# A new opening of the feed-forward layer, and another order in the tail, in a kernel of two attention and two feed-forward layers on one Trainium2 core

## The reference

```python
# end of attention 0: normalization of each head, scale, residual
h_norm = (h - mean) * rsqrt(var + 1e-05) * outnorm_scale      # 4 heads of 64
x = x + h_norm
# feed-forward 0, on the layer norm of x; act_qdq takes the largest |x| of the whole tensor
x = act_qdq(_layernorm(x))
up   = act_qdq(x @ lpbq_dequant(w_up).T)
gate = act_qdq(x @ lpbq_dequant(w_gate).T)
...
# experts: router on the layer norm of x, top 2 of 8, places by a running count
router_logits = einsum('gth,he->gte', x, w_router)            # 2 groups of 1024 tokens
gate, idx = top_k(softmax(router_logits), 2)
pos = cumsum(mask_kt, axis=1) * mask_kt - 1.0                 # capacity 160
y = combine(relu(expert_in @ wi) @ wo)
```

## Time and profile before

| | |
|---|---|
| median of 3 runs | 592.25 us (591.8 to 594.39) |
| the profiled execution | 594.54 us |
| its span, first to last instruction | 592.8 us |
| busy: TensorE, VectorE, ScalarE, GpSimd | 519.8, 381.6, 327.0, 142.5 us |
| mean granted TensorE clock | 0.952 |
| opening of feed-forward 0 | about 73 to 121 us |
| tail up to the first expert | about 393 to 425 us |

### The profile page before, as it was taken

One profiled execution on the slowest core, in us unless ns is written; L12 is line 12 of the kernel. 1 busy time (PEld: TensorE's weight loads), 2 busy tenths in 40 slices (PEclk: granted clock), 3 DMA queues, 4 the chain that ended last, 5 costly groups with the idle time before them and its releaser, 6 DMA issues.

```text
span 592.8 us, 9394 instructions
## 1 busy us (share of the span) xinstructions
PE 519.8 (88%) x3362; PEld 372.6 (63%) x3362; DVE 381.6 (64%) x980; ACT 327.0 (55%) x697; POOL 142.5 (24%) x202
## 2 busy tenths in 40 slices
PE   1989996899999700999999999998999999999994
PEld 1568864654444300887757678777788777677773
DVE  6576889845389989788688699987732232233101
ACT  2857577723389969680389799997122212211220
POOL 2006544000000000000332232211245344534441
PEclk9989999999999955699999999999799999999998
DMA  7910000000000000016000011014215645353410
GB/s 221 305 19 1 2 1 0 2 0 1 0 0 1 1 0 0 1 46 239 2 0 2 1 39 36 2 37 159 52 46 170 200 132 195 121 181 124 132 46 22
DMA packets 32013, 37.62 MB, mean 63 GB/s; under 512 B 8672, under 2 KB 27744, under 8 KB 31968
## 3 DMA queue, kind: packets, MB, share of 16 engines
q1 hardware_dynamic: 28896, 29.07, 15.3%
q0 software_dynamic: 3072, 7.95, 4.3%
HBM read 30.14 MB, written 6.88 MB: 62 GB/s over the span
## 4 chain that ended last, share of the span: by engine, by line
PE 71%; DVE 14%; ACT 9%; issue 2%; POOL 2%; POOLq 0%; DVEq 0%
PE pA L2203 12%; PE pB L2233 10%; PE pC L1869 6%; PE pC L1908 5%; PE pA L1902 3%; PE pB L1918 3%; PE pC L2217 3%; PE pA L1824 2%; PE pB L1824 2%; PE pC L1824 2%; ACT XIT L748 2%; DVE am L1259 2%; DVE arena L1255 2%; PE pB L1998 2%; DVE am L1225 2%
## 5 line engine op out<-in xcount | busy, mean ns | idle before, releaser
L499 POOL TENSOR_TENSOR arena<-KT,par 128x256 f32<-128x256 f32 x32 | 19.0, 615 | 248.6 <-DVE XIT L1333 186.7
L2203 PE MATMUL pA<-arena 128*128 128x320 f32 (+2 forms) x320 | 75.7, 387 | 0.5 <-ACT arena L923 0.5
L937 ACT ACTIVATE arena<-pA 128x320 f32<-128x320 f32 (+2 forms) x80 | 30.7, 384 | 73.0 <-PE pA L2203 67.5
L2203 PEld LDWEIGHTS pA<-arena 128*128 128x128 f32 x320 | 53.7, 190 | 16.2 <-issue 1.1
L2233 PE MATMUL pB<-arena 128*128 128x256 f32 x256 | 59.8, 385 | 0.0
L2233 PEld LDWEIGHTS pB<-arena 128*128 128x128 f32 x256 | 47.2, 190 | 8.5 <-issue 2.3
L1225 DVE TENSOR_REDUCE am<-arena 128x1 f32<-128x512 f32 x48 | 32.1, 682 | 23.0 <-ACT arena L688 22.9
L1869 PE MATMUL pC<-wdnT,XIT 128*128 128x256 f32 x192 | 43.5, 384 | 0.8 <-DVE XIT L1333 0.8
L1409 DVE TENSOR_REDUCE rm<-pA 128x16 f32<-128x2048 f32 x16 | 36.7, 2291 | 8.8 <-PE pA L1902 8.8
L1869 PEld LDWEIGHTS pC<-wdnT,XIT 128*128 128x128 f32 x192 | 36.5, 193 | 6.9 <-DVE XIT L1333 1.6
L1908 PE MATMUL pC<-ident,arena 128*128 128x128 f32 x240 | 35.4, 280 | 1.5 <-ACT XIT L784 0.8
(11 more groups left out here) (338 smaller groups left out, 1147.2 us busy)
## 6 DMA issues: line engine op xcount, KB each, us to landing
arena<-in_L_ffn_wi SPq DMA_DIRECT2D x8, 1024.0 KB, 5.2
arena<-in_L_ffn_wo SPq DMA_DIRECT2D x8, 1024.0 KB
X<-in_x SPq DMA_DIRECT2D x4, 512.0 KB, 5.7
arena<-in_ctx SPq DMA_DIRECT2D x4, 512.0 KB, 7.3
out<-X SPq DMA_DIRECT2D x4, 512.0 KB, 2.9
token_rows<-arena SPq DMA_DIRECT2D x4, 512.0 KB, 4.7
arena<-in_L_ffn_w_up SPq DMA_DIRECT2D x1, 768.0 KB, 7.5
arena<-in_L_ffn_w_gate SPq DMA_DIRECT2D x1, 768.0 KB, 9.2
```

The costliest lines, as they stand in the source:

```text
L937: nc.scalar.activation(HT[:, e % 2, f, n], ps[2 + f % 2][:, 0:n.stop - n.start], ACT.Relu).then_inc(s["h_relu"], 1)
L2203: last = mm(ps[2 + f % 2][:, 0:n.stop - n.start], WI[:, u, k, f * P:(f + 1) * P], XET[:, u, k, n], start=(k == 0), stop=(k == KD - 1))
```

## The change

In the opening: `head_scale(0)` comes before two `w_round` on VectorE; the fourth head of tiles 8 to 12 goes from VectorE to ScalarE (`ALL_HEADS` = 13); `values_kept(1)` and (2) come after tiles 4 and 9 in place of 6 and 14; `keys(2)` comes after the last head; two weight turns stand before the layer norm; four tiles (`NORM_ACT`) are normalized by ScalarE, by scale and bias; `TURN_BESIDE` is shorter, and the last two weight turns follow the spreading of the maximum, with four identity products instead of eight. In the tail: `d_back` comes directly behind `d_logits`, `d_turn(6)` and `d_turn(7)` earlier, `d_back4` behind `count(0)`; ScalarE takes the last roots and norms sooner; there are seven identity products in place of eleven.

```diff
-        TURN_BESIDE = (0, 2, 4, 5, 7, 8, 10, 11, 13)
+        TURN_BESIDE = (-1, -1, 1, 3, 5, 8, 11)
+
+        NORM_ACT = (4, 7, 10, 13)
 
         HB = NB // 2
+
+        ALL_HEADS = 13
@@ POOL h_scale
-                if b >= HB:
-                    pool.wait_ge(s["last_normed"], b - HB + 1)
+                if b >= ALL_HEADS:
+                    pool.wait_ge(s["last_normed"], b - ALL_HEADS + 1)
@@ ACT head_norm
-                for n in range(NH0 if b < HB else NH0 - 1):
+                for n in range(NH0 if b < ALL_HEADS else NH0 - 1):
@@ ACT, after the heads
-                if b == 13:
-                    keys(2)
+            keys(2)
+            keys(3)
+            weights_copy(4)
             rsqrt(4, NB)
-            keys(3)
+            weights_copy(5)
+
+            def xl_act(b):
+                if b == NORM_ACT[0]:
+                    act.wait_ge(s["xl_scale"], 1)
+                nc.scalar.activation(at(XL, b), at(X, b), ACT.Identity, scale=rstd[:, cols(b, 1)], bias=s2[:, cols(b, 1)]).then_inc(s["xl_act"], 1)
...
             for b in range(NB):
+                if b + 3 in NORM_ACT:
+                    xl_act(b + 3)
                 copy_x(b)
                 if b in TURN_BESIDE:
                     weights_copy(4 + TURN_BESIDE.index(b))
+            weights_copy(11)
+            weights_copy(12)
@@ ACT, tail
             norm4_act(8)
+            rsqrt(9, 4, 12)
             lt_copy()
             norm4_act(9)
-            rsqrt(9, 4, 12)
+            act.wait_ge(s["xr_ready"], 5)
+            norm4_act(12)
+            norm4_act(13)
             xt4(4)
             xt4(5)
+            norm4_act(14)
+            norm4_act(15)
+            xt4(6)
             lt4_copy()
-            act.wait_ge(s["xr_ready"], 5)
-            for b in range(12, NB):
-                norm4_act(b)
             exp4(0)
-            xt4(6)
             xt4(7)
@@ DVE, attention 0
+                if t == NB // 2:
+
+                    head_scale(0)
                 for b in (2 * t - 2, 2 * t - 1):
                     if b >= 0:
                         w_round(b)
-                if t == NB // 2:
-                    head_scale(0)
@@ DVE, opening
-                if HB <= t + 2 < NB:
+                if ALL_HEADS <= t + 2 < NB:
                     last_head(t + 2, 0, 0)
...
-                if t in (6, 14):
-                    values_kept(1 + t // 14)
+
+                if t == 4:
+                    values_kept(1)
+                if t == 9:
+                    values_kept(2)
...
             for t in range(NB + 1):
-                if t < NB:
+                if t < NB and t not in NORM_ACT:
                     xl(t, 0, 0)
+                if t == 1:
+                    V_.scalar_tensor_tensor(out=s2[:, 0:NB], in0=mean[:, 0:NB], scalar=-1.0, in1=rstd[:, 0:NB], op0=ALU.mult, op1=ALU.mult).then_inc(s["xl_scale"], 1)
@@ PE (turn3 and xl_max wait on xl_act for the tiles of NORM_ACT)
+            weights_turn(4)
+            weights_turn(5)
             for b in range(NB):
                 turn3(b)
                 if b in TURN_BESIDE:
...
-            pe.wait_ge(s["wtr_copied"], 13)
...
             whole_max(0, 1)
-            keep_busy(ps[1], 8)
+
+            weights_turn(11)
+            weights_turn(12)
+            keep_busy(ps[1], 4)
+            pe.wait_ge(s["wtr_copied"], 13)
@@ PE, tail
             d_logits()
+            d_back()
             d_turn(4)
-            d_back()
             d_turn(5)
             keep_busy(ps[7], 2)
+            d_turn(6)
             d_logits4()
+            keep_busy(ps[7], 2)
+            d_turn(7)
             keep_busy(ps[7], 3)
-            d_back4()
-            keep_busy(ps[7], 4)
...
-            d_turn(6)
-            keep_busy(ps[7], 2)
-            d_turn(7)
             count(0)
+            d_back4()
             for b in range(12, NB):
                 d_row(b)
```

More of the change, by code:

```diff
@@ L1200, in xl_max @@
             def xl_max(b, u, h):
-                dve.wait_ge(s["xl_ready"], b + 1)
+                if b in NORM_ACT:
+                    dve.wait_ge(s["xl_act"], NORM_ACT.index(b) + 1)
+                else:
+                    dve.wait_ge(s["xl_ready"], b + 1 - sum(r < b for r in NORM_ACT))
                 V_.tensor_reduce(am[:, 0, cols(b, 1)], at(XL, b), AX.X, ALU.max, apply_absolute_value=True).then_inc(s["xl_max"], 1)
             for t in range(NB + 1):
-                if t < NB:
+                if t < NB and t not in NORM_ACT:
                     xl(t, 0, 0)
+                if t == 1:
+                    V_.scalar_tensor_tensor(out=s2[:, 0:NB], in0=mean[:, 0:NB], scalar=-1.0, in1=rstd[:, 0:NB], op0=ALU.mult, op1=ALU.mult).then_inc(s["xl_scale"], 1)
                 if t >= 1:
@@ L1786, in turn3 @@
             def turn3(b):
-                pe.wait_ge(s["xl_ready"], b + 1)
+                if b in NORM_ACT:
+                    pe.wait_ge(s["xl_act"], NORM_ACT.index(b) + 1)
+                else:
+                    pe.wait_ge(s["xl_ready"], b + 1 - sum(r < b for r in NORM_ACT))
                 if b >= 2:
```

## The result

The changed kernel takes 588.65 us (median of nine runs, 587.62 to 591.66) against 592.25 (nine runs, 591.74 to 594.39): ratio 0.9933 [0.9917, 0.995]; the medians lie 3.6 us apart. The whole interval lies at or beyond the 0.5% that the prediction set as the bound, so the kernel is faster by it. Its profiled execution took 589.84 us with a span of 588.1, against 594.54 and 592.8.

A forecast was written before the change was run, and what follows sets the result against it. TensorE, busy 88%, was taken as the bound, so gains could come only where it waits: the feed-forward opening (2.5 us) and the tail (1.1), together 3.6 off 592.25, giving 588.65 us; range 587.2 to 590.9.

The forecast's parts named there:

- rival A: Whole kernel: gains come as summed, 588.65 us, own range 587.6 to 589.6; chance 0.50.
- Step (1): Opening: head_scale(0) ahead of two w_round; ScalarE's first head 1.8 us sooner, heads 3 and later 1.0 us sooner.
- no wait of ScalarE's variance beyond 0.3 us: Opening: a listed sign that the prediction is right, limiting ScalarE's wait for the variance to 0.3 us.
- Step (2): Opening: five fourth heads move to ScalarE, keys(2) behind the last head; last addition on VectorE 1.3 us sooner.
- Step (3): Opening: values_kept earlier, values(3) at full clock; ScalarE's keys and weight copy hidden by 0.2 us, first normalization 1.3 sooner.
- Step (4): Opening: four of 16 normalizations go to ScalarE; gain 1.2 us, ScalarE's tiles ready 1 to 2 us early.
- rival C: Opening: ScalarE becomes the limit, opening gives 1.2 us and tail 1.1; 590.0 us, chance 0.12.
- Step (5): Opening's end: last two weight turns behind the spread maximum, four identity products for eight; same length, ending with x_int(0).
- Rival B: Gate products: low clock there costs 1.7 us, leaving a gain of 1.9; 590.35 us, chance 0.27.
- Steps (6) and (7): Tail: last roots ahead of lt_copy and d_back ahead of d_turn(4); logits_0 0.95 us sooner.
- Steps (8) and (9): Tail: exp4(0) ready in time by 0.1 to 0.2 us, count(0) earlier; find_places(0) 1.1 us sooner in all.
- Rival D: Tail: low clock of 417 to 424 moves off the identity products, half of 2.9 us more; 587.2, chance 0.07.

The follow-up runs named there:

- scale_back: Changed kernel with head_scale(0) put back behind the two w_round; 589.2 us in its one run.
- ahead: Changed kernel with two more weight turns and their copies moved ahead of the layer norm; 594.23 us, ratio 0.9994 to the kernel before.
- back_only: Kernel before with only d_back moved directly behind d_logits; 592.92 us, ratio 0.9979.
- fill: Changed kernel with 13 identity products in TensorE's idle time ahead of the layer norm's first turn; 589.18 us, ratio 0.9908 to the kernel before.
- root_only: Kernel before with only the last rows' roots, rsqrt(9, 4, 12), moved ahead of lt_copy on ScalarE; 593.84 us, ratio 0.9991.
- tail_only: Kernel before with the tail of the changed kernel; 592.31 us, ratio 0.9941.
- norm_dve: Changed kernel with all sixteen layer-norm normalizations back on VectorE; 589.84 us, ratio 0.9934 to the kernel before.
- fill_three: Changed kernel with 13 identity products ahead of the layer norm's turns and three normalizations on ScalarE, not four; 589.53 us, ratio 0.9938 to the kernel before.

## Why the prediction was right, and where it was not

The time and the range held, and rival A came true as to mechanism. The sum did not: 2.5 + 1.1 should read 1.5 + 1.4, which is 2.9. The remaining 0.7 us of the 3.6 probably lies in the two stretches whose length hangs on the clock, since nothing else in the traces differs; that is argued and not shown. A part of the agreement is thus two errors that met, an opening summed 1.0 us too high, and against it a tail summed 0.3 too low and what the clock gave. That the median is the forecast to the hundredth is luck.

- Step (1) failed in its size. The mechanism held: VectorE's waits were gone, and ScalarE's first head came 1.84 us sooner after the first logarithm, against 1.8. But at the second half's logarithm 1.0 us was credited and 0.53 came, confirmed by scale_back. The step says that two-input operations are slow beside GpSimd and uses this for head_scale(0) alone; it did not ask what GpSimd would be doing during the variance once the heads come sooner. So ScalarE stood at `rsqrt(3)` for 1.50 us, where the step's own figures give 0.9. The sign "no wait of ScalarE's variance beyond 0.3 us" can't have meant this wait; at the layer norm's variance it held (ready at 103.81, logarithm at 103.84).
- Step (2) held in itself. The last head ended at the same place after the logarithm (27.63 before, 27.62 after), which is its sum with step (1)'s 0.53 put in: 1.66 - 1.14 - 0.53 = -0.01. The last addition came 0.88 us sooner, because `values_kept(2)` no longer stood ahead of it. The 1.3 of the forecast was too much by what step (1) lacked.
- Step (3) held: values(3) ran at full clock (3.62 us) and the layer norm's roots did not wait for them. The first normalization shifted by what the addition gave, 0.87.
- Step (4) was mis-sized. ScalarE was reckoned at 0.3 us for a normalization. Its rows show starts 0.49 us apart (111.39 to 111.88). Four are 2.0 us, not 1.2. That price stood in the prediction itself: step (8) takes 0.49 for this very shape, from four norms in 2.06 us. With the weight copies they fill the queue up to the last copy. VectorE's 1.2 us came as forecast; at the turn of the maximum 0.66 of them was left. This is rival C's mechanism, in part: the margin of "1 to 2 us" was not there. None of the listed signs of being wrong caught it: VectorE did not wait for `xl_act`; the loss came at the last copies.
- Step (5) held: turns and identity products behind the spread maximum ended with x_int(0), and the gate products followed 3.07 us behind the maximum, against 2.98.
- The clock: it did fall in the turning stage and was back for the gate products. Rival B did not occur in this trace; ahead and back_only show that it is real, and the spread of the changed kernel's runs (587.6 to 591.7) leaves room for it. That the low stretch "costs nothing, each tile has slack" was wrong by 0.2 us (fill).
- Steps (6) and (7) held to 0.02 us: 0.97 against 0.95, and back_only and root_only show that it takes both moves.
- Steps (8) and (9) were too careful: ScalarE reached `exp4(0)` at 409.61, 3.28 us behind logits_0, where I had allowed 3.65, so VectorE did not wait for it. `count(0)` began 4.21 us behind logits_0, as forecast (4.3), but find_places(0) followed it by 0.35 us, and not by the 0.6 of the sum. It is 0.46 us on top of logits_0's gain, not 0.15.
- Rival D was named for the low stretch of 417 to 424. Something like it occurs: 1.1 us less in this trace. But the twelve identity products ahead of `e_tokens(1)` took 2.91 us in both kernels; what got shorter are the four and the twelve behind them. The same holds for tail_only (8.54) and norm_dve (8.53), and not for fill_three (9.83). With eight short stretches in fourteen traces, root_only with the old tail among them, its chance should have been far above 0.07, for any kernel with this code, the kernel before as well.

## What to carry to other kernels

When work moves to an engine, take its price from start-to-start times of that very shape on that engine, and ask which queue ends last after the move: here VectorE gave up 1.2 us and ScalarE handed back half of it. When an edit lets an engine start sooner, list what its successors will now run beside. And compare traces by distances between events rather than by spans: 2.2 of 4.7 us lay in stretches that the change all but left alone.

## What the runs showed of the hardware

- The granted clock falls and rises at other places in executions of the same code. The price here is 1.1 us ahead of the down products, 1.4 at the gate products, 1.1 to 1.4 behind find_places(0); together more than either half of the change.
- A stretch that no edit touches varies most: from the start to the first heads' logarithm it took 70.62 us (scale_back) to 74.17 (root_only) in fourteen traces. Seven have a low clock from about 34 to 38 us, root_only to 41 (72.69 and more), the others have none there (72.86 and less).
- Twenty identity products without a gap (4.61 us) did not raise a low clock, and turns of 8.12 us in 10 left it at 0.50 for 20 us, while in the changed kernel it rose at 110.0 after turns alone; fourteen identity products (3.33 us from 236.02) were followed by a rise at 239.7 in one kernel, and by none until 246.1 in the other (3.33 us from 236.98). I did not settle what decides it.
- A VectorE operation of 128x32 with two inputs took 0.67 us beside a GpSimd operation, and 0.19 without.
